# Splitting all expert weights into bf16 pairs beside the attentions instead of inside the expert loop

## The reference

```
x = x + attention_0(layernorm(x), ctx)     # 16 heads, softmax over 128 context rows
x = x + ffn_0(layernorm(x))                # fake-quantised to 8 bits, gate/up/down, 704 wide
x = x + attention_1(layernorm(x), ctx)     # mLSTM: 4 heads, decay matrix from two gates
x = x + experts(layernorm(x))              # 8 experts, top 2 of them for each token

# experts:
probs = softmax(x @ gate_w);  weights, indices = top_k(probs, 2);  weights /= sum(weights)
for i in range(8):
    wi = where(indices == i, weights, 0).sum(-1)
    h = silu(x @ w1[i]) * (x @ w3[i])      # w1, w3: 256 x 1024
    out += (h @ w2[i]) * wi                # w2: 1024 x 256
```

## Time and profile before

| | us |
|---|---|
| median of 3 runs | 864.96 (863.54 to 866.54) |
| the profiled execution | 865.73 |
| its span, first to last instruction | 864.0 |
| PE busy in the span | 679.8 (79%) |
| DVE, ACT, POOL busy | 527.0, 410.6, 278.8 |
| HBM read, written | 145.90 MB, 11.80 MB |

### The profile page before, as it was taken

How to read it: one execution, slowest core, us unless ns; L and a number is a source line. 1 busy time by engine, 2 the same in 40 slices (tenths; PEclk the granted TensorE clock), 3 DMA queues, 4 the chain that set the end, 5 groups by cost and what they waited for, 6 DMA issues and landing times.

```text
span 864.0 us, 19336 instructions
## 1 busy us (share of the span) xinstructions
PE 679.8 (79%) x4571; PEld 471.9 (55%) x4615; DVE 527.0 (61%) x1371; ACT 410.6 (48%) x831; POOL 278.8 (32%) x390
## 2 busy tenths in 40 slices
PE   2999999885853991577417989898989998989992
PEld 2788887663322670466404556565656555655661
DVE  5577789985867452788785464646454555464441
ACT  1466655556874463345225444545353545553430
POOL 3111111111436001644302263535354253553421
PEclk9799999986978795555558999999999999999996
DMA  8100000000000114211270514243331525431213
GB/s 260 32 13 12 16 14 13 0 1 1 0 0 12 44 42 159 87 28 27 97 245 19 169 30 132 67 128 73 105 90 31 170 34 165 124 73 24 34 22 110
DMA packets 45844, 58.41 MB, mean 68 GB/s; under 512 B 13497, under 2 KB 39417, under 8 KB 45273
## 3 DMA queue, kind: packets, MB, share of 16 engines
q1 hardware_dynamic: 38328, 47.79, 16.9%
q0 software_dynamic: 7488, 10.31, 7.2%
HBM read 145.90 MB, written 11.80 MB: 183 GB/s over the span
## 4 chain that ended last, share of the span: by engine, by line
PE 48%; DVE 18%; issue 14%; POOL 7%; DMA 3%; ACT 3%; DVEq 2%; POOLq 1%; ACTq 1%; SPq 0%
PE psum L995 16%; PE psum L1017 7%; PE psum L718 3%; PE psum L1008 3%; POOL region L658 3%; PE psum L702 3%; PE psum L725 3%; PE psum L895 2%; PE psum L738 1%; PE psum L757 1%; PE psum L707 1%; PE psum L840 1%; PE psum L888 1%; DVE region L1358 1%; DMA region<-xrow_dram,next_token 1%
## 5 line engine op out<-in xcount | busy, mean ns | idle before, releaser
L995 PE MATMUL psum<-region 128*128 x897 | 209.6, 382 | 19.8 <-POOL pause_p L660 6.2
L995 PEld LDWEIGHTS psum<-region 128*128 128x128 bf16 x936 | 91.6, 98 | 119.1 <-issue 30.4
L1017 PE MATMUL psum<-region 128*128 x936 | 112.5, 278 | 6.2 <-DVE region L1868 3.7
L1017 PEld LDWEIGHTS psum<-region 128*128 128x128 bf16 x936 | 91.3, 100 | 22.3 <-issue 9.2
L1261 ACT ACTIVATE region<-psum 128x512 f32<-128x512 f32 x78 | 46.5, 596 | 115.0 <-PE psum L995 104.2
L1838 DVE TENSOR_TENSOR region<-psum,region 128x512 f32<-128x512 f32 x78 | 53.9, 690 | 72.9 <-ACT region L1261 62.9
L628 POOL TENSOR_TENSOR pause_p<-minus_half 128x1 f32<-128x1 f32 x37 | 7.1, 193 | 191.4 <-DVE next_token L1854 190.6
L640 POOL DMA_INDIRECT sum_dram<-region,tok_idx x39 | 62.0, 1589 | 6.6 <-issue 6.3
L1282 ACT ACTIVATE pause_a<-one_col 128x1 f32<-128x1 f32 x117 | 23.7, 202 | 84.1 <-issue 70.2
L525 POOL TENSOR_TENSOR region<-region,pair_mask 128x256 f32<-128x256 f32 x32 | 18.9, 612 | 137.8 <-ACT region L1062 137.8
L1868 DVE TENSOR_TENSOR region<-psum,region 128x1024 bf16<-128x1024 f32 x39 | 47.6, 1222 | 20.1 <-ACT region L1269 20.1
(11 more groups left out here) (304 smaller groups left out, 1386.0 us busy)
## 6 DMA issues: line engine op xcount, KB each, us to landing
region<-in_L_ffn_w SPq DMA_DIRECT2D x117, 1024.0 KB
region<-in_ctx SPq DMA_DIRECT2D x48, 128.0 KB, 2.1
region<-neg_max_dram SPq DMA_DIRECT2D x4, 1024.0 KB, 7.6
xrow_dram<-region SPq DMA_DIRECT2D x1, 2080.0 KB, 7.8
x_sb<-in_x SPq DMA_DIRECT2D x4, 512.0 KB, 7.1
sum_dram<-x_sb SPq DMA_DIRECT2D x1, 2048.0 KB, 7.5
region<-in_L_ffn_w_down SPq DMA_DIRECT2D x1, 704.0 KB, 8.1
region<-in_L_ffn_w_gate SPq DMA_DIRECT2D x1, 640.0 KB, 8.6
```

Source lines behind the costliest of these rows:

```text
L995: last = mm(psum[:, 2 * f + n, :], (xT_lo if xl else xT_hi)[:, p, k, :], weights_at(place, wl, n, k * F1 + f * FH, FH), start=(i == 0), st ...
L1017: last = mm(psum[:, 7, 0:D], (hT_lo if hl else hT_hi)[:, f, :], weights_at(place, wl, 2, f * D, D), start=(i == 0), stop=(i == 3 * (F1 // ...
```

## The change

No expert weight is split inside the expert loop any more.

**Early parts.** The 18 matrices of experts 2 to 7 are split during the first attention. They pass through a ring of three buffers in `region2` (not in use before the feed-forward stage). SP loads the fp32 matrix; ACT casts the high part in four pieces of 512 columns, two in the middle of a batch step and two at its end (`high_chunks`); POOL subtracts the low part in four pieces behind `mask_k` (`split_part`); SP stores the pair of 1024 KB to a DRAM tensor `split_dram`. Of matrices 15, 16 and 17 the casts stand behind the batch loop. DVE and POOL wait for all stores before they write the hidden values of the feed-forward stage over the ring.

**Late parts.** The six matrices of experts 0 and 1 are split after the feed-forward stage, by POOL alone (four casts, four subtractions each), right into slots 0 and 1. Those of expert 1 are also stored to DRAM.

**Expert loop.** SP's program is written out tile by tile. It reads slot, expert and a flag from `tile_info` and loads each pair straight into its slot on that condition, gate and up once PE is through with those of tile t-3, down once PE is through with the down of tile t-4. The flag is zero where experts 0 and 1 are already in their slots. ACT, DVE and POOL have no weight work left there.

**Beside that.** The loops of the first attention are written out on ACT, POOL and SP. The context loads of the second attention move from SP to ACT (`front_c`). ACT loads its silu table before the expert loop. The first presets of the second attention count on another semaphore. `gates_all` moves to another part of `region2`. Three small DVE instructions compute the new flag, and one DVE copy in the statistics becomes a reduction over a dimension of one.

```diff
+        late_at = (5 * pair_words, 6 * pair_words + B * P + 2 * KT * P)
+        split_dram = nc.dram_tensor("split_dram", (E, 3, P, 2 * PART), BF16, kind="Internal").ap()
+
+        def ring_of(i):
+            return i % 3
+
+        def uses(i):
+            return i // 3 + 1
+
+        def part_of(i):
+            return (2 + i // 3, i % 3) if i < EARLY_PARTS else ((i - EARLY_PARTS) // 3, i % 3)
+
+        def whole_part(i):
+            if i < EARLY_PARTS:
+                return early_ring[:, ring_of(i), 0:PART], early_ring[:, ring_of(i), PART:2 * PART].bitcast(BF16)
+            at = late_at[i % 2]
...
+            def load_part(i):
+                view, width = weight_part(i)
+                if i >= (2 if i < EARLY_PARTS else EARLY_PARTS + 2):
+                    sp.wait_ge(part_split, i - 1)
+                sp.dma_start(whole_part(i)[0].rearrange("p (t f) -> p t f", f=width), view).then_inc(part_loaded[ring_of(i)], 16)
+
+            def store_part(i):
+                sp.wait_ge(part_split, i + 1)
+                e, n = part_of(i)
+                sp.dma_start(split_dram[e, n, :, :], whole_part(i)[1]).then_inc(part_stored[ring_of(i)], 16)
+
...
-                    sp.dma_start(ctx_sb[:, p, :], ctx_in[2 * i + (p + 2), :, :]).then_inc(ctx_loaded[p], 16)
+            load_part(0)
+            load_part(1)
+            for i in range(EARLY_PARTS + 1):
+                if i + 2 < B:
+
+                    sp.wait_ge(t1_done, i + 1)
+                    sp.dma_start(ctx_sb[:, i % 2, :], ctx_in[i + 2, :, :]).then_inc(ctx_loaded[i % 2], 16)
+                if i >= 1:
+                    store_part(i - 1)
+                    if i + 1 < EARLY_PARTS:
+                        load_part(i + 1)
...
-                    sp.dma_start(ctx_c[:, p, :], ctx_in[2 * i + (p + 2), :, :]).then_inc(cctx_loaded[p], 16)
+            load_part(EARLY_PARTS)
+            load_part(EARLY_PARTS + 1)
+            for i in range(EARLY_PARTS, PARTS):
+                if part_of(i)[0] == 1:
+                    store_part(i)
+                if i + 2 < PARTS:
+                    load_part(i + 2)
 
             sp.wait_ge(gates_read, B)
             for n in range(2):
...
+                return slot, expert, need
+
+            def load_matrix(n, info, signal):
+
+                slot, expert, need = info
+                sp.dma_start(expert_w[:, bass.ds(slot + n * 2 * PART, 2 * PART)],
+                             split_dram.rearrange("e n p c -> p e n c")[:, bass.ds(expert, 1), n, :].rearrange("p e c -> p (e c)"),
+                             cond=(need > 0)).then_inc(signal, 16)
+
+            for t in range(NT + 1):
+                if t < NT:
+                    info = info_of(t)
+                    if t >= 1:
+                        sp.wait_ge(gate_up_loaded, 32 * t)
+                    if t >= 3:
+
+                        sp.wait_ge(gu_done, 2 * t - 4)
+                    load_matrix(0, info, gate_up_loaded)
+                    load_matrix(1, info, gate_up_loaded)
+                if t >= 1:
+                    if t >= 2:
+                        sp.wait_ge(down_loaded, 16 * (t - 1))
+                    if t >= 4:
+
+                        sp.wait_ge(dn_done, t - 2)
+                    load_matrix(2, info_before, down_loaded)
+                info_before = info
+            sp.wait_ge(down_loaded, 16 * NT)
...
+            def split_part(i):
+                whole, pair = whole_part(i)
+                pool.wait_ge(part_loaded[ring_of(i)], 16 * uses(i))
+                chunks = [slice(c, c + CHUNK) for c in range(0, PART, CHUNK)]
+                if i >= EARLY_PARTS:
+                    pool.wait_ge(part_split, i)
+                    for c in chunks:
+                        nc.gpsimd.tensor_copy(pair[:, c], whole[:, c]).then_inc(part_high, 1)
+                for n, c in enumerate(chunks):
+                    if i >= EARLY_PARTS:
+                        pool.wait_ge(part_high, (i - EARLY_PARTS) * len(chunks) + n + 1)
+                    elif n == 0:
+                        pool.wait_ge(part_cast[ring_of(i)], uses(i))
+                    last = nc.gpsimd.tensor_tensor(pair[:, PART:2 * PART][:, c], whole[:, c], pair[:, c], ALU.subtract)
+                last.then_inc(part_split, 1)
+
...
+            for b in range(2, B):
+                mask_k(b, b % 2)
+                split_part(b - 2)
 
 
             for n, part in enumerate((slice(0, EARLY), slice(EARLY, B))):
+                if n == 1:
+                    split_part(B - 2)
+                    split_part(B - 1)
                 pool.wait_ge(ln2_eps, n + 1)
                 nc.gpsimd.tensor_tensor(rstd[:, part], rstd[:, part], minus_half[:, part], ALU.pow).then_inc(rstd2_ready, 1)
+            split_part(B)
+            split_part(B + 1)
+
+            for r in range(3):
...
-            nc.gpsimd.memset(q_only, 0.0).then_inc(q_preset, 1)
-            nc.gpsimd.memset(v_c, 1.0).then_inc(q_preset, 1)
+            nc.gpsimd.memset(q_only, 0.0).then_inc(v_preset, 1)
+            nc.gpsimd.memset(v_c, 1.0).then_inc(v_preset, 1)
+            for i in range(EARLY_PARTS, PARTS):
...
+            def high_chunks(i, first, count):
+                whole, pair = whole_part(i)
+                if first == 0:
+                    act.wait_ge(part_loaded[ring_of(i)], 16 * uses(i))
+                    if i >= 3:
+                        act.wait_ge(part_stored[ring_of(i)], 16 * (uses(i) - 1))
+                for n in range(first, first + count):
+                    c = slice(n * CHUNK, (n + 1) * CHUNK)
+                    last = act_fn(pair[:, c], whole[:, c], ACT.Copy)
+                if (first + count) * CHUNK == PART:
+                    last.then_inc(part_cast[ring_of(i)], 1)
...
+                if b >= 1:
+                    high_chunks(b - 1, 0, 1)
                 exps(b, 0)
-                if inner or b + 1 < B:
+                if b >= 1:
+                    high_chunks(b - 1, 1, 1)
+                if b + 1 < B:
                     qk_copy(b + 1, 1 - p)
                 probsT_copy(b, 1)
+                if b >= 1:
+                    high_chunks(b - 1, 2, 2)
 
...
             outT_copy(B - 1)
+            high_chunks(B - 1, 0, 4)
             act.wait_ge(ot_done, B)
             act_fn(oT[:, :, :], bank7[:, 0:KT, :], ACT.Copy).then_inc(oT_ready, 1)
+            high_chunks(B, 0, 4)
 
 
             act.wait_ge(fw_loaded, 112)
             act_fn(clip[:], clip[:], ACT.Exp, scale=-1.0).then_inc(clip_exp, 1)
+            high_chunks(B + 1, 0, 4)
             act.wait_ge(wT_done, 1)
             for q in range(3):
...
 
-            def front_c(b, p):
+            def front_c(b, p, more=True):
                 act.wait_ge(ct_done, b + 1)
+                if more:
+                    act.dma_start(ctx_c[:, p, :], ctx_in[b + 2, :, :]).then_inc(cctx_loaded[p], 16)
+                if not isinstance(b, int) or b >= 2:
+
...
 
-            def weights_high(n, t, p, loads, inner=False):
-
-
-
-                place = act.value_load(tile_info[0:1, 1, bass.ds(t, 1)], min_val=0, max_val=(SLOTS - 1) * SLOT)
-                new = act.value_load(tile_info[0:1, 2, bass.ds(t, 1)], min_val=0, max_val=1)
-                if inner or t >= 1:
-
-                    act.wait_ge(part_high[n], t)
-
-                act.wait_ge(part_loaded[n][p], 16 * loads)
-                act_fn(pause_a[:, 3 + n:4 + n], one_col[:], ACT.Copy)
-                with act.If(new > 0):
-                    act_fn(expert_w[:, bass.ds(place + n * PART, PART)], stage[:, p, n, :], ACT.Copy)
-                act_fn(pause_a[:, n:n + 1], one_col[:], ACT.Copy).then_inc(part_high[n], 1)
-
-            def tile_step(t, p, pair, inner=False):
+            def tile_step(t, p, inner=False):
 
...
 
+            for r in range(3):
+                dve.wait_ge(part_stored[r], 16 * EARLY_PARTS // 3)
             hidden(0, first=True)
             with dve.Fori(1, G) as g:
                 hidden(g)
...
-            nc.vector.tensor_copy(tile_info[:, 0, :], te)
-            nc.vector.tensor_copy(tile_info[:, 1, :], tslot)
-            link_d(nc.vector.tensor_copy(tile_info[:, 2, :], tchg))
+            link_d(tt(tneed, te, tcum, ALU.not_equal))
+            link_d(nc.vector.scalar_tensor_tensor(tneed, tcum, 1.5, tneed, ALU.is_ge, ALU.max))
+            link_d(tt(tneed, tneed, tchg, ALU.mult))
...
-            def weights_low(n, t, p, inner=False):
-
-                place = dve.value_load(tile_info[0:1, 1, bass.ds(t, 1)], min_val=0, max_val=(SLOTS - 1) * SLOT)
-                new = dve.value_load(tile_info[0:1, 2, bass.ds(t, 1)], min_val=0, max_val=1)
-                if inner or t >= 1:
-
-                    dve.wait_ge(part_low[n], t)
-
-                dve.wait_ge(part_high[n], t + 1)
-                nc.vector.memset(pause_d[:, 3 + n:4 + n], 0.0)
-                with dve.If(new > 0):
-                    tt(expert_w[:, bass.ds(place + (3 + n) * PART, PART)], stage[:, p, n, :],
```

(6 more changed lines are left out.)

155 lines of the change are left out of this document (58 added, 97 removed).

## The result

The changed kernel takes 900.91 us (median of 4 runs, 898.68 to 903.13) against 865.43 beside it on the same chip: ratio 1.0408, 95% interval 1.0382 to 1.0434. The forecast had the direction and missed the size by almost three times: +12.5 us said, about +36 measured.

A forecast was written before the change was run, and what follows sets the result against it. PE was taken to bound the expert loop and fill the first attention. Terms -28 + 13 + 5 + 3 + 11.5 + 8 = +12.5 gave 877.5 us, likeliest range 867 to 891, wider range 856 to 899.

The forecast's parts named there:

- Expert loop, -28: Tiles 0 to 37: 37 tiles at 9.22 us, 341.1 instead of 369.3 us; bounds -30 and -24.
- the bound of 30.0: Expert loop: PE stands still for 30.0 us, the most that taking work off other engines can give.
- ACT's casts in the steps, 0: First attention: casts of 512 columns fit ACT's gaps at no cost, at most 0.1 us a step.
- Context rows, +13: First attention: contexts late behind stores and loads, 10.5 us from stalls every second step, 2.5 for batch 2; bounds 0 and 29.
- S + 12.05: First attention: when PE wants the next context, counted from S, the start of a batch's first scores.
- Clock, +3: First attention: one of six stalls lowers PE's clock and costs 3 us; bounds 0 and 17.
- the stalls pull the clock down: Rival, first attention: each stall of 2 us costs another 2.8, +17 instead of +3, 891 us; chance 0.13.
- DVE behind POOL, +5: First attention: DVE's norm waits for a running POOL piece, 0.45 us a step, taken as 5; bounds 0 and 16.
- Casts behind the last batch, +11.5: Behind the first attention: ACT waits for loads 16 and 17, first quantised group at 217.9 instead of 206.34; bounds 8 and 16.
- Late parts, +8: Ahead of the gates: their DMA goes late behind the store that waits for POOL's splits; bounds 0 and 18.
- a sign of being wrong: Gates: a gate DMA that waits for DVE as before, instead of being released by POOL's split.
- everything else: All outside the four compared stretches of the profile: forecast 0, measured +2.3 us.

The follow-up runs named there:

- e1: The changed kernel with the first attention's context rows issued by ACT instead of SP; 864.97 us, ratio 1.0055 to the kernel before.
- e4: e1 with POOL's early subtractions 8 columns wide instead of 512, the other low parts left out; 858.61 us, ratio 0.9985 to the kernel before.
- e8: e7 with POOL's late casts and subtractions in pieces of 256 columns instead of 512; 870.10 us, ratio 1.0061 to the kernel before.
- e5: e1 with the early loads issued one place earlier, three ahead of the loop; 862.19 us, ratio 0.9998 to the kernel before.
- e7: e5 with POOL's early subtractions in 16 pieces of 128 columns instead of 4 of 512; 859.51 us, ratio 0.9958 to the kernel before.
- e12: e5 with only two of the six late matrices loaded, POOL's work and the stores kept; 859.73 us, ratio 1.0016 to the kernel before.
- e13: e7 with SP issuing each early load ahead of the store instead of behind it; 859.32 us, ratio 1.0011 to the kernel before.

## Why the prediction was wrong

- *Expert loop, -28:* measured -22.3, outside its bounds. The loads come in time and the gaps at expert changes go, as said. The term was mis-sized by the 9.22 us for every tile: the mean is 9.38. Every fourth lasts 9.6 to 9.8 where PE's loop turns, which is over half of the 5.9 us missed; the first lasts 10.0, and the others a little over 9.22. PE still stands idle for 12.9 us in the stretch, not under 3; that the gain is 22.3 all the same comes from 5.2 us less of busy time, which the bound of 30.0 had not counted. The row was one of the shorter tiles. The turn's cost was in the trace of before, in tiles without a new expert.
- *ACT's casts in the steps, 0:* about right. With contexts on ACT (e1) and tiny subtractions (e4) the stretch is 157.6 against 157.7, casts included.
- *Context rows, +13:* the mechanism and the place were right, shown by e1, and every second step stalls up to batch 11. The size was wrong, 18.5 us by PE's waits for `in_ctx` alone, and more than half of the miss is batch 2: 6.7 instead of 2.5. Its context landed 8.4 us after its issue (33.96) behind two loads, where 2.1 + 4.9 had been reckoned, and PE stood in front of it from 35.8 on, so nearly all of it was lost. The regular stalls were four of 2.9 us in the mean and one of 0.2, 11.8 in all, instead of 5.5 of 1.9. The price of a turn in the queue held: 7.1 - 2.1 = 5.0 us for two transfers, against 2 x 2.46. Missing was SP's own time, for the context is issued 0.87 us behind the store and landed 8.4 us behind it in the sample instead of 7.0; and PE wanted it at S + 11.7, not S + 12.05.
- *Clock, +3:* the step that failed most. I let one stall in six lower the clock; the trace shows 0.50 behind all five long ones and behind the two late waits of 2.06 and 4.26 us, and PE's busy time is 15.7 us longer. The rival "the stalls pull the clock down" had this and was given 0.13. The earlier trace rows had shown one wait with its price, and the reason against it (waits of 1 us that cost no clock) speaks of waits a third as long. Waits and clock together made 38.5 us where the two terms had 16.
- *DVE behind POOL, +5:* measured 2.3 in the attention (e4 against e1), inside its bounds; in the changed kernel itself PE's wait of 4.26 us for DVE comes on top, where DVE's weight preparation fell beside a split. Missed was the same effect behind the last batch: there it takes DVE's norms from 3.9 to 10.7 us. The Trainium skill (SBUF — State Buffer, "SBUF: two separate sides") has one side holding the ports for a whole instruction; norms spaced by exactly one POOL piece agree. That a DVE instruction can stand while 28 POOL instructions go by (e8) it does not say.
- *Casts behind the last batch, +11.5:* measured +14.7. ACT's waits for loads 16 and 17 are there (1.21 and 3.10 us), but e5 removed them and gained nothing: the norms' chain is as long. Only both together (e7) gave 5. The total came out near the forecast, but the forecast had ACT's path alone.
- *Late parts, +8:* measured +3.6, and the cause was another, so that it lies inside its bounds is luck. SP's last store behind POOL's splits goes at 380.5, and the gates' DMA at 382.41, behind DVE's last copy (382.11), as before. A cast of 512 columns takes 0.62 us, under both prices given for it (0.75 and 0.769). The 3.6 us go away with four of the six loads (e12), and with them PE's wait of 2.2 us for context rows. So the gates' DMA waits for DVE as before, which the prediction had named as a sign of being wrong. The store ahead of it probably costs 0.9 us: the gates' step of the chain of waits is 3.75 us where it was 2.87, part of the 2.3 us of "everything else".

## What to carry to other kernels

Before a big transfer that waits for something is added to a program, list the small ones behind it that somebody waits for, and issue those from a place that waits only for their own buffer: one moved DMA was worth 30 us here. Do not count on another queue to make them land sooner; give them lead. Price a stall of PE at its wait plus the half clock behind it; in this first attention that held for all seven of 2.06 to 6.7 us. Where VectorE works SBUF to SBUF beside GpSimd, count its instructions and let each cost one GpSimd instruction. And when two chains end within a few microseconds of each other, repair both before judging either.

## What the runs showed of the hardware

- A context transfer of 128 KB alone took 2.0 to 2.1 us. In the queue of the big ones it took 7.1 us behind a store and a load of 1024 KB and 5.0 behind a load. On the other queue it took 6.7 us issued soon after two loads, 3.5 (e7) and 4.9 (e13) about 4 us after a store and a load, and 2.1 (e1) at 5.8 us after the load; with loads close behind one another the median was 3.2 and two on the chain of waits took 4.93 and 6.12.
- A GpSimd subtraction costs 1.16 us for 512 columns and 0.39 for 128, so shorter pieces cost 6.3 us for a matrix instead of 4.6. Casts: 0.62 us for 512 columns, 0.41 for 256.
- VectorE's norms beside them start one per GpSimd instruction. Its row maxima from PSUM kept their 1.22 us.
- A VectorE instruction on 32 columns, 0.34 us in e7, stood for 10.79 us beside short GpSimd instructions issued back to back; others of 4 columns stood for 4.98 and 3.85 us.
- PE's turn of a loop cost 0.6 us with 4 tiles in its body and 4.2 to 4.7 with 12.
